# Four layers on one 4096 x 4096 matrix: the products of a step's high half go first, and the wait for its low half stands before the last third

## What is computed

```python
x = _layernorm(x + _L0_gnn_ref(x, adj, adj, W1, f1, W2, f2))      # twice adj @ (adj @ (x W)), with a filter between
x = _layernorm(x + concat([x, adj @ x]) @ weight)
# L2: logits = q @ k.T / scale + bias; gates = sigmoid(logits) * adj * adj
#     x = _layernorm(x + layernorm(relu(concat([x, gates @ messages]) @ W_upd + b_upd)) * gamma + beta)
# L3: twice swish((adj @ x) @ W + b)
x = _layernorm(x + _L3_gnn_ref(x, adj, W, b))
```

## Time and profile before

| | us |
|---|---|
| median of three runs | 1713.41 (1713.12 to 1714.25) |
| span of the profiled execution, first to last instruction | 1712.5 |
| PE busy in it | 1622.0 (95%) |
| DVE busy in it | 1280.4 (75%) |
| ACT busy in it | 1103.1 (64%) |

### The profile page before, as it was taken

One profiled execution on the slowest core, in us unless ns is written; L12 is line 12 of the kernel. 1 busy time (PEld: TensorE's weight loads), 2 busy tenths in 40 slices (PEclk: granted clock), 3 DMA queues, 4 the chain that ended last, 5 costly groups with the idle time before them and its releaser, 6 DMA issues. The chain is left out here.

```text
span 1712.5 us, 18888 instructions
## 1 busy us (share of the span) xinstructions
PE 1622.0 (95%) x7618; PEld 761.2 (44%) x7618; DVE 1280.4 (75%) x1423; ACT 1103.1 (64%) x757; POOL 11.3 (1%) x25
## 2 busy tenths in 40 slices
PE   7999999999999999999999999899998899999996
PEld 4444444444444444444444444343444344444442
DVE  6876546653766498649996898989899996455997
ACT  5766847674786586656666677676767666445663
POOL 2000000000000000000000000000000000000000
PEclk9999999999999999999999999999999999999998
DMA  9979789977999789978677364454545797665892
GB/s 365 412 299 398 297 360 391 369 292 323 368 400 412 268 303 414 385 273 316 249 289 276 123 216 164 161 197 162 185 170 211 285 377 287 239 243 194 343 334 113
DMA packets 68423, 490.76 MB, mean 287 GB/s; under 512 B 7824, under 2 KB 7984, under 8 KB 9328
## 3 DMA queue, kind: packets, MB, share of 16 engines
q1 hardware_dynamic: 67104, 485.00, 74.1%
q0 software_dynamic: 1088, 4.49, 0.7%
q10 hardware_dynamic: 144, 0.07, 0.0%
HBM read 420.32 MB, written 69.21 MB: 286 GB/s over the span
## 5 line engine op out<-in xcount | busy, mean ns | idle before, releaser
L903 DVE SCALAR_TENSOR_TENSOR a_lo<-a_ring,a_hi 128x2048 f16<-128x2048 f32 x332 | 752.1, 2288 | 306.6 <-ACT a_hi L709 306.5
L709 ACT ACTIVATE a_hi<-a_ring 128x2048 f16<-128x2048 f32 x332 | 629.4, 1906 | 337.0 <-PE spare L531 195.2
L531 PE MATMUL acc<-a_hi,y_hi 128*128 128x512 f16 x1584 | 478.0, 383 | 58.2 <-DVE a_lo L903 35.4
L531 PE MATMUL acc<-a_hi,y_lo 128*128 128x512 f16 x1584 | 477.9, 383 | 0.0
L531 PE MATMUL acc<-a_lo,y_hi 128*128 128x512 f16 x1584 | 477.2, 382 | 0.0
L531 PEld LDWEIGHTS acc<-a_hi,y_hi 128*128 128x128 f16 x1584 | 152.9, 98 | 254.0 <-DVE a_lo L903 43.4
L531 PEld LDWEIGHTS acc<-a_lo,y_hi 128*128 128x128 f16 x1584 | 155.6, 98 | 191.1 <-issue 6.6
L531 PEld LDWEIGHTS acc<-a_hi,y_lo 128*128 128x128 f16 x1584 | 155.6, 98 | 190.3 <-issue 5.3
L924 DVE SCALAR_TENSOR_TENSOR gates<-gates,a_ring 128x1024 f32<-128x1024 f32 x128 | 155.9, 1218 | 29.4 <-ACT gates L738 29.0
L721 ACT ACTIVATE a_hi<-gates 128x1024 f16<-128x1024 f32 x128 | 134.8, 1053 | 64.4 <-DVE gates L924 64.2
L911 DVE TENSOR_TENSOR a_lo<-gates,a_hi 128x1024 f16<-128x1024 f32 x128 | 155.8, 1217 | 0.0
(11 more groups left out here) (98 smaller groups left out, 671.9 us busy)
## 6 DMA issues: line engine op xcount, KB each, us to landing
a_ring<-adj_dram SPq DMA_DIRECT2D x332, 1024.0 KB, 7.4
saved_squares<-squares SPq DMA_DIRECT2D x64, 1024.0 KB, 12.3
a_ring<-saved_squares SPq DMA_DIRECT2D x64, 1024.0 KB, 4.8
x_T<-xt_dram SPq DMA_DIRECT2D x4, 512.0 KB, 8.1
x_rows<-x_dram POOLq DMA_DIRECT2D x1, 2048.0 KB, 12.1
out_dram<-x_rows POOLq DMA_DIRECT2D x3, 512.0 KB, 4.0
out_dram<-x_rows SPq DMA_DIRECT2D x2, 256.0 KB, 2.0
w<-W_dram POOLq DMA_DIRECT2D x2, 64.0 KB, 5.4
```

Source lines behind the costliest of these rows:

```text
L531: mm = pe.matmul(sums[:, h * BANK:(h + 1) * BANK], blk(y[:, y_pass % 2, :], j), slot(a, st)[:, s, h * BANK:(h + 1) * BANK], start=(begins ...
L709: act.activation(slot(a_hi, st), loaded(st), ACT.Copy, scale=2.0 ** A_EXP).then_inc(s_ahi, 1)
L903: dve.scalar_tensor_tensor(out=slot(a_lo, st).rearrange("p s c -> p (s c)"), in0=loaded(st).rearrange("p s c -> p (s c)"), scalar=2.0 ** A ...
```

## The change

The three products of a unit are taken apart. First come, for each of the unit's blocks, `y_hi` and `y_lo` with `a_hi` (8 matmuls of a whole step, 4 of a gated unit, 4 of a half step at the end); then `y_hi` with `a_lo` (4, 2 and 2). The wait at the head of a unit is now for the high half, and a wait for the low half stands between the two parts. PE raises a new semaphore `s_hi_used` after the high part. ACT waits for that one before it refills a high slot, and also for the old content's low half having been made (DVE reads the high slot for it). DVE gets a wait of its own for `s_unit` before it overwrites a low slot. The number of matmuls, weight loads, splits and transfers stays the same.

```diff
+        def low_half_made(eng, n, s):
+
+            if STREAM[n].p == GATED:
+                eng.wait_ge(s_glo, gated_index(STREAM[n], s) + 1)
+            else:
+                eng.wait_ge(s_alo, PLAIN_BEFORE[n] + 1)
...
+            def high_products(unit, halves=range(HALVES)):
...
+                for s in blocks_in(unit):
+                    begins = unit.first and s == (unit.s or 0)
+                    for y in (y_hi, y_lo):
+                        for h in halves:
+                            mm = pe.matmul(sums[:, h * BANK:(h + 1) * BANK], blk(y[:, y_pass % 2, :], st.j0 + s),
+                                           slot(a_hi, st)[:, s, h * BANK:(h + 1) * BANK],
+                                           start=(begins and y is y_hi), stop=False)
+                return mm
...
                 if st.p == GATED:
-                    u = gated_index(st, unit.s)
-
-                    pe.wait_ge(s_glo, u + 1)
+                    pe.wait_ge(s_ghi, gated_index(st, unit.s) + 1)
                 elif FIRST_USE[st.n] == n:
-                    pe.wait_ge(s_alo, PLAIN_BEFORE[st.n] + 1)
+                    pe.wait_ge(s_ahi, PLAIN_BEFORE[st.n] + 1)
...
-                for s in range(SJ) if unit.s is None else [unit.s]:
-                    mm = product(unit, s)
-                mm.then_inc(s_unit, 1)
+                high_products(unit).then_inc(s_hi_used, 1)
+                if st.p == GATED:
+                    pe.wait_ge(s_glo, gated_index(st, unit.s) + 1)
+                elif FIRST_USE[st.n] == n:
+                    pe.wait_ge(s_alo, PLAIN_BEFORE[st.n] + 1)
+                low_products(unit).then_inc(s_unit, 1)
...
                 if st.n >= RING:
-                    act.wait_ge(s_unit, freed(st))
+                    act.wait_ge(s_hi_used, freed(st))
+                    low_half_made(act, st.n - RING, SJ - 1)
...
                 act.wait_ge(s_g, u + 1)
-                act.wait_ge(s_unit, slot_free(u))
+                act.wait_ge(s_hi_used, slot_free(u))
+                low_half_made(act, st.n - RING, u % SJ)
...
             def split_low(st):
                 dve.wait_ge(s_ahi, PLAIN_BEFORE[st.n] + 1)
+                if st.n >= RING:
+                    dve.wait_ge(s_unit, freed(st))
...
             def gate_low(u):
                 dve.wait_ge(s_ghi, u + 1)
+                dve.wait_ge(s_unit, slot_free(u))
```

More of the change, by code:

```diff
@@ L244, in build @@
         s_ahi, s_alo, s_unit = sem("a_hi_ready"), sem("a_lo_ready"), sem("unit_multiplied")
+        s_hi_used = sem("high_half_multiplied")
         s_lg, s_pr = sem("logits_ready"), sem("probs_ready")
@@ L519, in _, with blocks_in @@
             at = 0
-            def product(unit, s, halves=range(HALVES)):
+            def blocks_in(unit):
+                return range(SJ) if unit.s is None else [unit.s]
+            def high_products(unit, halves=range(HALVES)):
                 st = unit.step
@@ L525, in product, with low_products @@
                 sums = acc[:, st.k % 2, :] if unit.use == "own" else spare[:, :]
[L526 to L529, removed]
+                for s in blocks_in(unit):
[6 more added lines that the diff above has]
+                return mm
+            def low_products(unit, halves=range(HALVES)):
+                st = unit.step
+                y_pass = st.p - 1 if unit.use == "own" else st.p
+                sums = acc[:, st.k % 2, :] if unit.use == "own" else spare[:, :]
+                for s in blocks_in(unit):
                     for h in halves:
-                        mm = pe.matmul(sums[:, h * BANK:(h + 1) * BANK], blk(y[:, y_pass % 2, :], j),
-                                       slot(a, st)[:, s, h * BANK:(h + 1) * BANK],
-                                       start=(begins and t == 0), stop=(ends and t == 2))
+                        mm = pe.matmul(sums[:, h * BANK:(h + 1) * BANK], blk(y_hi[:, y_pass % 2, :], st.j0 + s),
+                                       slot(a_lo, st)[:, s, h * BANK:(h + 1) * BANK],
+                                       start=False, stop=(unit.last and s == SJ - 1))
                 return mm
@@ L591, in half_step @@
                 if h == 0:
+                    pe.wait_ge(s_ahi, PLAIN_BEFORE[unit.step.n] + 1)
+                high_products(unit, [h])
+                if h == 0:
                     pe.wait_ge(s_alo, PLAIN_BEFORE[unit.step.n] + 1)
-                for s in range(SJ):
-                    mm = product(unit, s, [h])
-                return mm
+                return low_products(unit, [h])
             def project_half(h):
```

## The result

| | before | after |
|---|---|---|
| median of the runs, us | 1713.55 (1713.12 to 1714.25, 4 runs) | 1703.61 (1702.36 to 1704.89, 4 runs) |
| ratio | | 0.9939, interval 0.9925 to 0.9952 |
| span of the profiled execution, us | 1712.5 | 1700.8 (its own time: 1702.63) |

The change made the kernel 9.9 us faster. The forecast was 15.4 (1698), so it was right in sign and 5.6 us too low in time. Both profiles are used here, and the difference between them turns out to be the point of this case.

A forecast was written before the change was run, and what follows sets the result against it. PE, busy 95% of the span, was taken as the bound, with 58.1 us of low-half waits as ceiling. Gains of 16.5 us less 1.5 for the clock took 1712.5 to 1697.5; plus 0.9 to the median, 1698 us, range 1688 to 1707.

The forecast's parts named there:

- the first 300 us, behind the start: Program start: the first unit waits for `a_lo`, but the third projection's `y_lo` depends on a load's landing: 0.
- 454.73: PE's 2.36 us wait for `z_T`, behind ACT work begun by a wait for PE, moves with the earlier refill: 0.9 us.
- start of pass 7: DVE idles twice behind ACT, which waits for PE; the split at 1331.94 comes earlier: 0.9 us.
- 1368.01: PE's 3.70 us idle before its 250 us stream in pass 7; high products done in the wait gain 1.7 us.
- pass 8 without its tail: Two chunks, limited by `z_T` behind three splits; only DVE's own idle time, 0.7 each, can be won: 1.4 us.
- the clock: Longer idle before projections halves PE's clock; one to two such drops, about 1.3 us each on the path: -1.5 us.
- The halved sum: Rival: only direct waits with a stream behind them count, 8.2 us, so 1705; chance 0.13.
- every wait counts: Rival: all long, short and gated waits give their full gain, 34 us, so 1679; chance 0.05.
- Satisfied waits: 0: The 460 added waits on PE cost nothing when already satisfied; upper bound 0.10 us each, 46 us.
- DVE's new wait: 0: DVE's wait for `s_unit` asks for a unit four steps back, finished before DVE can be ready: 0.
- the clock takes it: Rival: every lengthened idle stretch drops PE's clock, 8 x 1.3 = 10 us, so 1703 to 1708; chance 0.11.
- The signs named ahead: Among them: a chunk of pass 6 takes as long as before, one of pass 8 falls from 30.5 to about 29.8.

The follow-up runs named there:

- first profile: Profiled execution of the changed kernel in its first timing against the kernel before: span 1700.8 us, median of the runs 1703.61 us, ratio 0.9939.
- the late wait alone: Changed kernel, but ACT and DVE wait as in the kernel before, so ACT refills a high slot only after the whole unit: 0.9937 of the kernel before.
- the kernel with two waits: Changed kernel's order of products, PE waiting for the low half at the unit's head and again in mid-unit, ACT and DVE as before: 1.0000 of the kernel before.
- the early refill alone: Changed kernel with its new order and ACT's early refill, but PE waits for the low half at the unit's head, none in mid-unit: 0.9967 of the kernel before.
- the kernel with three places filled: Changed kernel plus matmuls by zero weights before the three projections at 24.0, 649 and 798 us: 0.9891 of the kernel before.
- the second profile: Profile of the same changed kernel, run again beside the follow-up experiments: span 1697.6 us, ratio 0.9923 to the kernel before.
- the first comparison: First timing of the changed kernel against the kernel before: 1703.61 us against 1713.55, ratio 0.9939.
- the second: The changed kernel timed again, unaltered, beside the follow-up experiments on the same chip: 0.9923 of the kernel before.
- The filled kernels: Kernels with zero-weight matmuls in PE's long idle stretches: changed kernel 0.9884, kernel before 0.9960, only the late wait 0.9919, only the early refill 0.9924.
- fewer fills: Changed kernel with zero matmuls at its long idle stretches, except those inside pass 6 (units 366, 398, 430) and at unit 457: 0.9887 of the kernel before.

## Why the prediction was right, and which term was off

Each term of the sum against the shift of the units in the first profile:

| term | forecast | measured |
|---|---|---|
| the first 300 us, behind the start (281.79 above all) | 0 | 0.9 |
| 454.73 | 0.9 | 0.7 |
| 483.22 and 486.82 | 1.8 | 1.8 |
| three short waits for `z_T` | 1.5 | 1.7 |
| 707.57 | 1.7 | 1.7 |
| pass 5 | 2.8 | 3.0 |
| 920.40 | 0.8 | 0.8 |
| 954.83, and the rest of pass 6 | 0.9, 0 | 0.8, 0 |
| start of pass 7 | 0.9 | 0.9 |
| 1368.01 | 1.7 | 1.7 |
| pass 8 without its tail | 1.4 | 0.9 |
| tail | 2.1 | 2.0 |
| the clock | -1.5 | -5.4 |
| together | 15.0 | 11.6 (span: 11.7) |

The places at the start of pass 7 and at 1368.01 are read at the moment PE resumes and at unit 461, ahead of the loss to the clock there; pass 8 and the tail from the start of DVE's work in each. The sum is of unrounded values.

- **What bounds it.** Right. Tracing each wait to the stream behind it sized eleven of twelve places within 0.5 us; the waits for the low half fell by 31.4 us and the time by a third of that. The halved sum and "every wait counts" are both ruled out by the places at 225, 313 and 440.
- **The term missed.** Of its 0.9 us, 0.2 come near 91 us and 0.7 at 281.79, where PE waits for a `z_T` that passes over ACT. ACT's unbroken row of work ahead of it began with the landing of a load before, and with a wait for PE in the late wait alone:

```profile
268.08 1.91 ACT L709 ACTIVATE a_hi<-a_ring 128x2048 f16<-128x2048 f32 x1 [1.12 <-DMA a_ring<-adj_dram]
```

```profile
268.76 1.91 ACT L734 ACTIVATE a_hi<-a_ring 128x2048 f16<-128x2048 f32 x1 [0.68 <-PE acc L554]
```

  The late wait alone and the kernel with two waits have no early refill, and they win 0.44 us there all the same; by this the load landed late in the one profile of before. The early refill can claim the rest, 0.2 to 0.7 us in the two profiles and in the early refill alone, and nothing in the kernel with three places filled. So the mechanism of 454.73 is at most part of this term.
- **Satisfied waits: 0.** Right: 1.0000 with 460 of them. The rule that I weighed against the change, that a wait in mid-unit could stop the pulling ahead of weight loads, doesn't decide anything here.
- **DVE's new wait: 0.** Right, though DVE's waits in the first profile seem to say otherwise: they put three idle stretches of its splits down to PE, the longest up to 480.00. The same one stood in the profile before, put down to ACT (DVE after, DVE before, ACT after):

```profile
DVE a_lo L932 <- PE acc L554: 3.7, 3, 2.2
```

```profile
480.00 2.29 DVE L932 SCALAR_TENSOR_TENSOR a_lo<-a_ring,a_hi 128x2048 f16<-128x2048 f32 x1 [2.21 <-PE acc L554]
```

```profile
480.87 2.29 DVE L903 SCALAR_TENSOR_TENSOR a_lo<-a_ring,a_hi 128x2048 f16<-128x2048 f32 x1 [2.21 <-ACT a_hi L709]
```

```profile
478.07 1.90 ACT L735 ACTIVATE a_hi<-a_ring 128x2048 f16<-128x2048 f32 x1
```

  The high half is made at 478.07 + 1.90 = 479.97, and PE's unit ends within 0.05 us of it; so it is at the other two places. DVE waited for the high half, and the new wait added at most 0.04 us. A view names whoever came last, if only by that much.
- **Where the 5.6 us lie.** 3.3 are in the spans (15.0 us forecast, 11.7 measured), mainly 3.9 of the clock and 0.5 of pass 8 too much, less the 0.9 missed. Another 1.9 are in the distance from the profiled span to the median, which I had kept at 0.9 and which was 2.8 after: every time is 1.8 us above its own span (1702.63 and 1700.8), but the profiled execution was the slowest of its kernel before (1714.25) and one of the two fast ones after. The rest is rounding.
- **The clock, -1.5: mis-sized**, the largest part of it. The mechanism was named (a gain at a low half lengthens the idle time before a projection, and the clock falls) with 1.3 us a drop and one to two drops. By the shifts the first profile lost 1.7 at the start, 1.1 at 649, 1.8 at 798 and 1.0 more at 1358: 5.4 (the last is 1.66 instead of 2.6 won between units 440 and 463). Two things were wrong. I took no drop at the start, where PE's wait for `y_lo` grew from 1.2 to 2.5 us. And I reckoned with a fixed set of drops, which the traces refute: the second profile has none at 798, 929 and 949, ends 3.2 us earlier, and its net loss to the clock is about 2. So the term itself differs by 3.2 us between two executions of one program, and a single trace of before could not give it more closely than that.
- **The rival "the clock takes it"** (1703 to 1708) has the number of the first comparison, 1703.6, which lies just outside the forecast's own 1693 to 1703; the second, 0.9923 of 1713.5, is 1700.3 and inside. It has the mechanism in part: projections do drop the clock, but the places behind the late waits in pass 6 pay nothing (7.05 us won at units 408 and 440, on both sides of a drop).
- **The signs named ahead.** A chunk of pass 8 takes 29.73 us from one `z_T` on DVE to the next (1616.90 to 1646.63; forecast 29.8), a chunk of pass 6 95.8 us from one `val` to the next (95.9 before).

What remains open: which of the idle stretches drop the clock in a given execution. The filled kernels show that keeping PE at work stops most drops, and not every one: with fewer fills PE still waits 2.03 us at 24.08, behind 8 zero matmuls, and the clock is at half from 25.3 on. That unfilled kernels differ by the drops that they happen to have is read from the traces; only the filled ones test it.

## What to carry to other kernels

A wait that is moved behind independent work is worth what the stream behind it gains: follow each wait to the next thing that holds the engine (here a third of the waits' sum was time). Two kernels that differ by a few us can differ by their clock drops alone. Before a part of a change is called useless by its time, lay the traces side by side unit by unit, or keep PE at work in both and compare again. Where PE is in step and must wait a few us, matmuls by zeros in the wait, kept shorter than it, gained 6 us here by keeping the clock.

## What the runs showed of the hardware that was not expected

- A drop comes behind an idle stretch as short as 1.91 us (1647.90), and not behind the same 1.91 us at 1618.17 in the same execution.
- One drop costs 1.1 to 1.8 us where PE is in step (two between units 313 and 376: 3.3 us). Inside pass 6 it costs nothing behind the late waits (1162.00, 1257.60) and 0.9 us at 1093.70.
- A semaphore wait in mid-sum that is already satisfied costs PE at most 0.0034 us.
